# Row norms of a transformer layer: one power instruction instead of two, three small steps on VectorE instead of four on GpSimd, and another order for the row scatters

## What is computed

```python
def _L0_attn_ref(x, w_qkv, w_proj, q_norm_w, k_norm_w):      # heads: 16 x 16
    q, k, v = (qkv[0], qkv[1], qkv[2])
    q = _rms_norm(q, q_norm_w); k = _rms_norm(k, k_norm_w)
    q, k = _rope(q, k, cos, sin)
    attn = softmax(causal(q @ k.T * scale))
    return (attn @ v) @ w_proj.T

def _L0_ffn_ref(hidden_states, norm_weight, router_w, ...):
    var = jnp.mean(jnp.square(hidden_states), axis=-1, keepdims=True)
    normed = hidden_states * jax.lax.rsqrt(var + 1e-08) * norm_weight
    shared = jnp.maximum(normed @ sw1 + sb1, 0.0) @ sw2 + sb2
    probs = jax.nn.sigmoid(flat @ router_w.T)
    scores, idx = jax.lax.top_k(probs, TOPK)
    ...
    return shared + routed.reshape(b, s, -1)

x = _layernorm(x + _L0_attn_ref(x, ...), axis=-1)
x = _layernorm(x + _L0_ffn_ref(x, ...), axis=-1)
```

## Time and profile before

| | |
|---|---|
| median of 3 runs | 956.29 us (954.79 to 958.54) |
| profiled execution | 957.52 us, span of the profile 955.8 us |
| TensorE busy | 896.0 us (94% of the span) |
| VectorE, ScalarE, GpSimd busy | 576.6, 615.3, 457.2 us |
| mean granted TensorE clock | 0.984 of full speed |

### The profile page before, as it was taken

How to read it: one execution, slowest core, us unless ns; L and a number is a source line. 1 busy time by engine, 2 the same in 40 slices (tenths; PEclk the granted TensorE clock), 3 DMA queues, 4 the chain that set the end, 5 groups by cost and what they waited for, 6 DMA issues and landing times.

```text
span 955.8 us, 26112 instructions
## 1 busy us (share of the span) xinstructions
PE 896.0 (94%) x9049; PEld 693.3 (73%) x9050; DVE 576.6 (60%) x1152; ACT 615.3 (64%) x1060; POOL 457.2 (48%) x668
## 2 busy tenths in 40 slices
PE   4789999998999989999999999999999999999995
PEld 1444555555555546888889989989899889898885
DVE  8655698889888636784344444454444433428875
ACT  4788898888878766442656655556655453667753
POOL 5344557877878636572134444344434343412211
PEclk9799999999999989999999999999999999999998
DMA  5112223433212255567882122121212121248641
GB/s 175 67 68 95 94 101 106 158 114 135 101 58 84 69 176 194 202 204 266 267 292 74 50 67 70 52 68 55 67 56 67 46 68 47 74 145 269 214 160 44
DMA packets 68706, 112.76 MB, mean 118 GB/s; under 512 B 7728, under 2 KB 46000, under 8 KB 68496
## 3 DMA queue, kind: packets, MB, share of 16 engines
q1 hardware_dynamic: 51248, 77.32, 24.5%
q10 hardware_dynamic: 10896, 16.40, 5.9%
q0 software_dynamic: 6480, 17.97, 5.2%
HBM read 66.58 MB, written 45.08 MB: 117 GB/s over the span
## 4 chain that ended last, share of the span: by engine, by line
PE 76%; ACT 7%; DVE 6%; issue 4%; POOL 2%; DMA 2%; another core or an unknown queue 1%; ACTq 1%; DVEq 0%; SPq 0%; POOLq 0%
PE hb L1811 23%; PE yb L1827 23%; PE pv_bank L1599 6%; PE slot L1577 4%; PE ma L1612 4%; PE slot L1586 3%; PE hb L1665 3%; ACT prob L872 2%; PE mb L1747 2%; PE ma L1622 1%; PE tr L1685 1%; DMA rs<-resid 1%; PE yb L1702 1%; PE mb L1735 1%
## 5 line engine op out<-in xcount | busy, mean ns | idle before, releaser
L1042 ACT ACTIVATE hf<-hb,b 128x256 f32<-128x256 f32 (+1 forms) x392 | 155.0, 454 | 206.2 <-PE hb L1811 200.7
L1811 PE MATMUL hb<-xgT,wts 128*128 128x256 f16 (+1 forms) x1872 | 213.2, 263 | 1.4 <-ACT hf L1042 1.2
L1827 PE MATMUL yb<-wts,hh 128*128 x1704 | 210.5, 273 | 0.9 <-DVE hh L1454 0.9
L1454 DVE TENSOR_TENSOR hh<-hf,hh 128x1024 f16<-128x1024 f32 (+1 forms) x98 | 120.2, 1229 | 137.3 <-ACT hh L1047 105.4
L1811 PEld LDWEIGHTS hb<-xgT,wts 128*128 x1872 | 181.2, 98 | 20.3 <-ACT hf L1042 1.0
L807 POOL DMA_INDIRECT y_tok<-yb,dest x71 | 77.8, 1096 | 227.0 <-DVE yb L1466 216.9
L1827 PEld LDWEIGHTS yb<-wts,hh 128*128 128x128 f16 x1704 | 166.3, 98 | 19.6 <-DVE hh L1454 1.2
L872 ACT ACTIVATE prob<-slot 128x1024 f32<-128x1024 f32 x160 | 161.6, 1034 | 27.8 <-PE slot L1586 27.3
L1047 ACT ACTIVATE hh<-hf 128x1024 f16<-128x1024 f32 (+1 forms) x98 | 97.6, 996 | 3.1
L741 POOL DMA_INDIRECT xg_rows<-xnh,sl_i x64 | 76.4, 1194 | 16.2 <-issue 13.9
L1577 PE MATMUL slot<-stk 64*128 64x128 f16 (+3 forms) x512 | 64.2, 308 | 16.2 <-ACT prob L872 11.6
(11 more groups left out here) (236 smaller groups left out, 1445.0 us busy)
## 6 DMA issues: line engine op xcount, KB each, us to landing
wts<-in_w_all SPq DMA_DIRECT2D x23, 512.0 KB
wts<-y_tok SPq DMA_DIRECT2D x32, 256.0 KB, 4.9
xg<-xg_rows ACTq DMA_DIRECT2D x30, 264.0 KB
stage<-in_w_all SPq DMA_DIRECT2D x12, 512.0 KB
w_split<-chunk_hl SPq DMA_DIRECT2D x12, 512.0 KB
xTf<-in_xT SPq DMA_DIRECT2D x8, 512.0 KB, 3.8
xin<-in_x SPq DMA_DIRECT2D x8, 512.0 KB
resid<-y SPq DMA_DIRECT2D x16, 256.0 KB
```

The source lines that it names most:

```text
L1042: act.activation(hf[:, c, 0:size], hb[c // 2][:, (c % 2) * TT:(c % 2) * TT + size], ACT.Relu, bias=bias, scale=1.0 / WS).then_inc(S("relu_ ...
L1454: dve.tensor_tensor(hh[:, par, 1, cs, 0:size], hf[:, cs, 0:size], hh[:, par, 0, cs, 0:size], ALU.subtract).then_inc(S("h_lo"), 1)
L1811: ins = pe.matmul(hb[hc // 2][:, (hc % 2) * TT:(hc % 2) * TT + size], weights(e, c, w, hc * P, P), xgT[:, par, x * DC + c, 0:size], start= ...
L1827: ins = pe.matmul(ybank[par][:, j * D:(j + 1) * D], hh[:, par, x, hc, P * j:P * j + P], weights(e, DC + hc * D // CH, w, hc * D % CH, D), ...
```

## The change

In `norms`, one GpSimd instruction now takes both powers: it reads columns 0 and 1 of `vv` and writes columns 4 and 5 (128 partitions x 2 tiles x 2 columns). For that the mean square must be there before the first power is taken. VectorE works it out from the variance alone, as variance / (variance + eps) + the other eps: a reciprocal, a multiplication and an addition behind the two small instructions that `added` had already, each waiting for the one before it. `var_ready` is given by the last of them. GpSimd keeps the shift. The readers take other columns.

The scatters of sequences 0 to 5 get other positions: (58, 60, 62, 66) for the first expert's four tiles in place of (58, 59, 61, 63), and (67, 68, 70, 72) for the second's in place of (64, 66, 67, 68). Sequences 6 and 7 keep theirs.

```diff
@@ -95,6 +95,8 @@
 RANK = (56,)
 SCATTER = (58, 59, 61, 63)
 SCATTER_2 = (64, 66, 67, 68)
+SPACED = (58, 60, 62, 66)
+SPACED_2 = (67, 68, 70, 72)
 STORE = (39, 43)
 STORE_XT = (43, 49)
 SPLIT_X = (-33,)
@@ -131,9 +133,9 @@
 
 def dispatch_position(c, t, k):
 
-    if k == 0:
-        return NPOS * c + SCATTER[t]
-    return NPOS * c + (SCATTER_2[t] if c < NB - 1 else SCATTER[-1])
+    if c >= NB - 2:
+        return NPOS * c + (SCATTER[t] if k == 0 else SCATTER_2[t] if c < NB - 1 else SCATTER[-1])
+    return NPOS * c + (SPACED if k == 0 else SPACED_2)[t]
 
 
 DISPATCHED = sorted(((c, t, k) for c in range(NB) for t in range(len(SCATTER)) for k in range(TOPK)),
@@ -714,19 +716,13 @@
                 def norms(c, u):
 
                     k = 2 * c + u + 1
-                    v = [vv[:, pair(u), i] for i in range(6)]
                     pool.wait_ge(S("var_ready"), k)
-                    pool.tensor_tensor(v[1], v[0], mhalf[:], ALU.pow).then_inc(S("norm_steps"), 1)
-                    pool.wait_ge(S("norm_steps"), 4 * k - 3)
+                    pool.tensor_tensor(vv[:, pair(u), 4:6], vv[:, pair(u), 0:2],
+                                       mhalf[:].unsqueeze(1).broadcast_to([P, 2, 2]), ALU.pow).then_inc(S("norms_ready"), 1)
+                    pool.wait_ge(S("norms_ready"), k)
                     pool.wait_ge(S("mean_neg"), k)
-                    pool.tensor_tensor(vv[:, pair(u), 6], v[1], mv[:, pair(u), 0], ALU.mult).then_inc(S("shift_made"), 1)
-                    pool.tensor_tensor(v[2], v[1], v[1], ALU.mult).then_inc(S("norm_steps"), 1)
-                    pool.wait_ge(S("norm_steps"), 4 * k - 2)
-                    pool.tensor_tensor(v[3], v[2], mv[:, pair(u), 1], ALU.mult).then_inc(S("norm_steps"), 1)
-                    pool.wait_ge(S("norm_steps"), 4 * k - 1)
-                    pool.tensor_scalar(v[4], v[3], FFN_EPS, None, ALU.add).then_inc(S("norm_steps"), 1)
-                    pool.wait_ge(S("norm_steps"), 4 * k)
-                    pool.tensor_tensor(v[5], v[4], mhalf[:], ALU.pow).then_inc(S("norms_ready"), 1)
+                    pool.tensor_tensor(vv[:, pair(u), 6], vv[:, pair(u), 4], mv[:, pair(u), 0], ALU.mult
+                                       ).then_inc(S("shift_made"), 1)
 
                 def scatter(c, t, k):
 
@@ -766,7 +762,7 @@
                     for t in (2 * u, 2 * u + 1):
                         pool.wait_ge(S("norms_ready"), 2 * c + u + 1)
                         pool.wait_ge(S("shift_made"), 2 * c + u + 1)
-                        pool.tensor_scalar(y0[:, t, :], y0[:, t, :], vv[:, t, 1:2], vv[:, t, 6:7], ALU.mult, ALU.add
+                        pool.tensor_scalar(y0[:, t, :], y0[:, t, :], vv[:, t, 4:5], vv[:, t, 6:7], ALU.mult, ALU.add
                                            ).then_inc(S("x1_done"), 1)
 
                 def step(g):
@@ -1216,10 +1212,16 @@
                         dve.wait_ge(S("y0_done"), 4 * c + t + 1)
                         dve.bn_aggr(mv[:, t, :], st6[:, t, :]).then_inc(S("mv_done"), 1)
                     dve.wait_ge(S("mv_done"), 4 * c + 2 * u + 2)
+                    k = 2 * c + u + 1
                     dve.tensor_scalar(vv[:, pair(u), 0], mv[:, pair(u), 1], LN_EPS, None, ALU.add
-                                      ).then_inc(S("var_ready"), 1)
+                                      ).then_inc(S("var_eps"), 1)
                     dve.tensor_scalar(mv[:, pair(u), 0], mv[:, pair(u), 0], -1.0, None, ALU.mult
                                       ).then_inc(S("mean_neg"), 1)
+                    dve.wait_ge(S("var_eps"), k)
+                    then(dve.reciprocal(vv[:, pair(u), 2], vv[:, pair(u), 0]), "var_rcp", k)
+                    then(dve.tensor_tensor(vv[:, pair(u), 3], vv[:, pair(u), 2], mv[:, pair(u), 1], ALU.mult), "sq_mean", k)
+                    dve.tensor_scalar(vv[:, pair(u), 1], vv[:, pair(u), 3], FFN_EPS, None, ALU.add
+                                      ).then_inc(S("var_ready"), 1)
 
                 def normalised(c, u):
```

## The result

The changed kernel takes 951.54 us (median of 20 runs), the kernel before 957.28 us in 20 runs beside it: a ratio of 0.9942, 95% interval 0.9932 to 0.9952, or 5.6 us less. One run of the changed kernel took 5058 us and is left out of the ratio. I forecast 953.7 us from a sum of 2.6 us, so the gain is about twice what I summed up. The profiled execution took 951.59 us, its span 949.9.

A forecast was written before the change was run, and what follows sets the result against it. TensorE was taken to bound the kernel, gaining only at its first-part waits: 1.0 + 0.8 + 0.8 = 2.6 us off 957.5 gives 954.9, or a median of 953.7 us; range 948.8 to 958.5.

The forecast's parts named there:

- What bounds the kernel: Whole kernel: TensorE is busy 896 of 956 us; gain at most what it loses in the first part to what changes.
- GpSimd saves 2.0 us: GpSimd's small norm steps, first power to row norm: 3.69 us become 1.65; saving 2.0 us, or 1.6 with a dear power.
- VectorE pays 0.64: Three new dependent VectorE steps ahead of `var_ready` make it and GpSimd's start 0.64 us later.
- Stage 0, 1.0 us: Sequence 0's scatter stage: `nat_low` starts 1.0 us earlier, TensorE's 1.41 us wait falls to 0.4; gain 1.0 us.
- Stage 1, 0.8 us: Sequence 1's stage: `nat_low` up to 1.15 us earlier, capped by ScalarE's 0.45 us wait, plus TensorE's 0.34; gain 0.8 us.
- Sequences 2 and 3, 0 us: Stages of sequences 2 and 3: ScalarE's own queue and work bind, so gain 0.
- Sequences 4 to 6, 0 us: No q and k to prepare; GpSimd waits for VectorE at each norm and TensorE needs the rows later; gain 0.
- The last norm, 0.8 us: Sequence 7, half 1, near 401 us: the norm's 3.61 us become 2.83; gain 0.8 us, 0.4 with a dear power.
- The spaced scatters, 0 us: Scatter positions are only an order; slack of 1.8 us against some 1.4 us ahead of TensorE's transposes; cost 0.
- Hidden: Rival, chance 0.17: ScalarE's exponentials bind everywhere and VectorE gains nothing; gain about 0.4 us, 955.9 us.
- More than the sum: Rival, chance 0.19: VectorE's unexplained 4.76 us stretch ending at 345 us also goes; gain 7.4 us, 948.9 us.
- The scatters in the way: Rival, chance 0.14: moved scatters meet VectorE's work and delay GpSimd's cast and copies in four stages; slower, 962.7 us.

The follow-up runs named there:

- the norms alone: Changed kernel with all scatters at the positions of the kernel before, on a 952 us chip; ratio 0.9952 to the kernel before.
- second profile: The unchanged kernel before, run and profiled once more on another chip; median 951.8 us.
- group 3: Third of four groups of runs, on a chip of its own; the kernel before had a median of 951.8 us, the changed kernel a ratio of 0.9940.
- group 1: First group of runs, chip not on record; the kernel before had a median of 957.3 us, the changed kernel a ratio of 0.9942.
- 952 us chip: Chip of the second and third groups of runs, where the kernel before had medians of 951.9 and 951.8 us.
- 957 us chip: Chip of the first and fourth groups of runs, where the kernel before had medians of 957.3 and 957.5 us.
- the kernels with late copies: Changed kernel, old positions in sequences 0 to 3: 0.9975. Changed kernel, all old positions, GpSimd's first bias addition two scatters earlier: 0.9970.
- first profile: The profile of the unchanged kernel before from which the forecast was made; that execution took 957.5 us.
- changed again: The changed kernel, unaltered, run once more beside the kernel before on another chip; ratio 0.9940.
- before again: The kernel before, unaltered, run and profiled once more on another chip; median 951.8 us.

## Why the prediction came out as it did

- *The time.* 951.54 us is 2.2 us below the forecast of 953.7 and inside the range of 948.8 to 958.5, but that range also held no change at all (956.3), so the time alone says little. The gain was more than twice the sum, and what was missing is in the terms below. My narrower low end of 951.7 had 1.0 us "from sequences 2 and 3, should ScalarE's queue follow", and that did come, with 1.8 us; its other 1.0 us, a power without contention at the last norm, did not.
- *What bounds the kernel* held. Nearly every gain lies at TensorE's waits for the bank that `averaged` frees and for `mh`; the exception is stage 4.
- *GpSimd saves 2.0 us*: 1.6 us (3.69 to 2.12), the dear end of my range. (L729, my lower bound, had three VectorE instructions of 128x64 beside it, not nothing.) *VectorE pays 0.64*: 0.6.
- *Stage 0, 1.0 us*: 0.93 changed, 0.99 with the norms alone. The size was right, the way was not: `nat_low` does not start earlier. The idle time is eaten by one stretched instruction, and the time comes back from those behind it that are no longer stretched. That the two are nearly even, 1.66 against 1.80 us, is luck: the forecast did not know of either.
- *Stage 1, 0.8 us*: 1.34, and 1.14 with the norms alone, which is my own 1.15 for `nat_low` without the cap. The step that failed is the cap "after which it is bound by its own work" from ScalarE's 0.45 us. The second profile has 1.09 us in its place, which is nearly the whole gain of the norms alone; the 0.45 was what a stray delay of 0.64 us had left of it. TensorE's wait for ScalarE behind it is as long as before (1.34 against 1.32 us) and only lies earlier.
- *Sequences 2 and 3, 0 us*: 0.66 and 1.12 in group 3. The step that failed is "the 1.54 us at 268.84 are ScalarE's own queue". The second profile shows 0.78 us of it, and the VectorE wait of 0.48 us that was hidden. At 308.40 the argument was the cap of stage 1 again, and here it fails by the second profile's numbers too: ScalarE's root step waited 0 and 0.16 us for VectorE in the two sequences, and the stages gained 0.66 and 1.12 us. ScalarE waits for TensorE's scores in turn (0.34 us at 305.92), so that the two moved together is likely; no run isolates it.
- *Sequences 4 to 6, 0 us*: right for the norm. The 0.7 us of stage 4 in group 3 are ScalarE's DMA issue (1.29 against 0.58 us), the 0.3 us in group 1 the difference of the two stretches "remote" (4.76 against 4.47 us); stage 5 has -0.09.
- *The last norm, 0.8 us*: 1.24. Half 1 gives 0.61, less than forecast, since the wide power there took 1.94 and not 1.69 us. The step that failed is to count half 1 alone: half 0's norm holds VectorE 1.53 us ahead of half 1's `y`.
- *The spaced scatters, 0 us*: right by themselves (1.0002); with the norms on a 952 us chip the ratios do not part (0.9952 against 0.9940), and the trace has 1.0 us, 0.64 of it in stage 5, where additions and subtractions meet. Wrong on a 957 us chip: there stages 0 to 3 gained 4.2 us with the new positions and 0.5 to 0.8 us with the old ones (against the before of group 1). The late copies cost before itself next to nothing (0.16 us in stage 2), because TensorE waited for VectorE anyway; that the shorter norm takes this cover away is the likely reason for the rest, but the kernels with late copies also have them in stages 0 and 1, where before has none. I costed the spacing at nothing without asking what it costs once another part of the change has taken that cover.
- *The rivals.* "Hidden" (955.9) is excluded in both groups that ran the changed kernel. "More than the sum" was nearer in the gain (7.4 us, the sum 2.6, measured 5.6), but its mechanism is wrong: the 345 us stretch is in all six profiles of 957 us chips, changed or not, and in none of the eight others. "The scatters in the way" had the sign wrong: where positions counted, the old ones did harm.

## What to carry to other kernels

Take a second profile before a wait is called an engine's own: a stray delay of 1 us in one execution can cover the wait that counts, or shorten the one that you take as a cap (0.45 us in the first profile, 1.09 in the second). When GpSimd and VectorE work side by side, a change of one shifts which instructions meet, and a step's price is that of its neighbours too: list for each large VectorE instruction what tensor instruction of GpSimd lies beside it, before and after. Judge parts of a change together, for what costs nothing while something else is waited for can count once that is gone. Where kernels differ in a stage that the change does not touch, read the queues too: here one DMA issue of ScalarE made 0.6 to 0.8 us.

## What the runs showed of the hardware

- One tensor instruction of GpSimd of 1.3 us beside a VectorE instruction with f16 output stretched this by more than its own length: the subtraction into `hh` 2.87 instead of 1.23 us, and a cast in the last norm 2.18 instead of 0.43 us (a scatter of 1.10 us ran beside the cast's start). Which of the two is stretched differs: in changed again the wide power, started 0.19 us behind a subtraction, took 1.94 us (1.04 at its shortest), and the subtraction its 1.22.
- Scatters beside VectorE instructions with two SBUF inputs stretched nothing (1.21 us for the chunk split beside 2.09 us of scatter, 0.69 for `nat_low` beside 1.49); beside the cast into `xnh` one of 0.99 us made 0.43 us into 0.66.
- The issue of the same DMA on ScalarE's queue took 0.46 to 0.58 us in three profiles and 1.21 to 1.39 us in five, and stage 4 changed with it.
- The same kernel is 5.5 us slower in some groups than in others, 4.6 us of it in stage 4, by stretches in which VectorE or ScalarE stands for a releaser that the trace calls "remote", with scatters beside or just ahead of it in the places read here: 4.0 to 4.8 us near 345 us in six of six profiles there, 3.30 us at a copy into `stk`, 1.13 us at `lg`. Eight profiles on the other chips have none before 470 us. The name alone is no sign of it: at 435.21 of the first profile it stands at a wait of ScalarE of 7.99 us, for which before again names VectorE (8.17 us). What the engines wait for is open.
